# First attention of a decoder block: where the check of a top-32 selection is counted, and when sums are copied out

## The reference, cut to what matters

```python
Q = (x_text @ Wq).reshape(Bb, Tt, H, DH)          # 16 x 256 queries, 4 heads
K = (x_vision @ Wk).reshape(Bb, Gg, H, DH)        # 1601 keys
scores = jnp.einsum('bthd,bghd->bhtg', Q, K) / np.sqrt(DH).astype(np.float32)
topv, topi = jax.lax.top_k(scores, K_TOP)         # K_TOP = 32
probs = jax.nn.softmax(topv, axis=-1)
attn = jnp.zeros_like(scores).at[bi, hi, ti, topi].set(probs)
attn_mean = attn.mean(axis=1)                     # mean over the heads
V = x_vision @ Wv
c_t = jnp.einsum('btg,bgd->btd', attn_mean, V)    # then two FiLM products
```

## Time and profile before

| | us |
|---|---|
| median of 3 runs (lowest, highest) | 2802.61 (2799.21, 2804.65) |
| the profiled execution | 2799.72 |
| its span from first to last instruction | 2798.0 |
| PE, DVE, ACT, POOL busy over the span | 2382.1, 2183.1, 2102.0, 1531.4 |
| mean granted TensorE clock | 0.917 |

### The profile page before, as it was taken

One profiled execution on the slowest core, in us unless ns is written; L12 is line 12 of the kernel. 1 busy time (PEld: TensorE's weight loads), 2 busy tenths in 40 slices (PEclk: granted clock), 3 DMA queues, 4 the chain that ended last, 5 costly groups with the idle time before them and its releaser, 6 DMA issues. The chain is left out here.

```text
span 2798.0 us, 61626 instructions
## 1 busy us (share of the span) xinstructions
PE 2382.1 (85%) x19766; PEld 1236.7 (44%) x19766; DVE 2183.1 (78%) x7984; ACT 2102.0 (75%) x3544; POOL 1531.4 (55%) x2172
## 2 busy tenths in 40 slices
PE   7967888888888888865878849999999999999968
PEld 5634555555555555543542213333333333333348
DVE  8818888887888887834654579999999999999644
ACT  5739988988898998851522219999999989999935
POOL 1417778777787777752310043556556665543444
PEclk9968999988999999878978859999999999999989
DMA  8830000000000000018143023444443444433211
GB/s 246 266 102 1 14 14 16 23 14 16 14 14 14 14 14 14 14 50 290 31 63 85 20 73 96 95 108 107 107 104 98 102 99 98 104 88 55 74 46 45
DMA packets 163716, 199.26 MB, mean 71 GB/s; under 512 B 78966, under 2 KB 131740, under 8 KB 163376
## 3 DMA queue, kind: packets, MB, share of 16 engines
q1 hardware_dynamic: 153376, 157.34, 22.8%
q0 software_dynamic: 10000, 37.83, 3.9%
HBM read 133.22 MB, written 62.08 MB: 70 GB/s over the span
## 5 line engine op out<-in xcount | busy, mean ns | idle before, releaser
L2282 ACT ACTIVATE pb<-sps 128x512 f32<-128x512 f32 (+1 forms) x1664 | 897.9, 597 | 137.1 <-PE sps L2212 120.3
L2307 DVE TENSOR_REDUCE mx<-wps 128x2 f32<-128x1024 f32 x768 | 884.5, 1217 | 34.4 <-PE wps L2182 27.7
L1078 DVE MAX8 cand<-sc 128x8 f32<-128x46 f32 (+1 forms) x4480 | 603.0, 199 | 145.1 <-issue 82.1
L2227 PE MATMUL ops<-pb,va 128*9 128x256 f32 x6656 | 515.9, 382 | 9.5 <-issue 2.6
L854 PE MATMUL scores<-ctxT,qT 97*128 97x512 f32 (+1 forms) x1024 | 445.2, 584 | 81.5 <-ACT sc L966 69.5
L854 PEld LDWEIGHTS scores<-ctxT,qT 97*128 97x128 f32 x1024 | 208.6, 214 | 324.6 <-issue 224.7
L737 POOL TENSOR_TENSOR prf<-sc,prf 128x1601 f32<-128x1601 f32 x64 | 229.7, 3589 | 120.0 <-ACT prf L973 120.0
L737 POOL TENSOR_TENSOR prs<-sc,prs 128x1601 f32<-128x1601 f32 x64 | 230.7, 3604 | 18.6 <-ACT prs L973 15.7
L829 PE MATMUL misc<-diag,prs 128*128 128x128 f32 (+1 forms) x1664 | 227.8, 291 | 8.1 <-issue 6.9
L829 PEld LDWEIGHTS misc<-diag,prs 128*128 128x128 f32 (+1 forms) x1664 | 207.6, 199 | 18.5 <-issue 15.0
L2227 PEld LDWEIGHTS ops<-pb,va 128*9 128x9 f32 x6656 | 99.2, 88 | 253.6 <-ACT pb L2282 180.8
(11 more groups left out here) (476 smaller groups left out, 4233.6 us busy)
## 6 DMA issues: line engine op xcount, KB each, us to landing
FO<-keys SPq DMA_DIRECT2D x392, 50.0 KB
XX<-keys SPq DMA_DIRECT2D x392, 50.0 KB
ctxn<-in_ctx_dram SPq DMA_DIRECT2D x32, 576.0 KB
keys<-kpb POOLq DMA_DIRECT2D x42, 400.2 KB, 3.6
toep<-kernpad SPq DMA_DIRECT2D x8, 2048.0 KB, 15.0
values<-s_vs SPq DMA_DIRECT2D x16, 832.0 KB, 6.0
XX<-values SPq DMA_DIRECT2D x16, 832.0 KB, 4.7
keysf<-s_kf SPq DMA_DIRECT2D x16, 800.5 KB, 3.7
```

Source lines behind the costliest of these rows:

```text
L1078: st.add(v.max(cand[s % 2][:, 8 + n:8 + n + 7 * NP + 1:NP], sc[s % 4][:, c:c + w]))
L2227: ins = t.matmul(ops[VW * i:VW * i + DH1 + 1, 0:S], va[par][0:kn(kt), kt, 4 * g + i, :], pb[(UNITS * g + 2 * kt + i % 2) % 8][0:kn(kt), i ...
L2282: nc.scalar.activation(pb[(UNITS * g + u) % 8][0:rows_, :, :], sps[(UNITS * g + u) % SB][0:rows_, :, :], ACT.Exp).then_inc(p_ready, 1)
L2307: v.tensor_reduce(mx4[:, m // 2, :, 2 * g + m % 2, c], both, AX.X, ALU.max).then_inc(work_read, 1)
```

## The change

The sign pass on ACT is gone, and its buffers. DVE keeps three candidate buffers in place of two. After it has the threshold of slot j, it counts for slot j-1: how many of the 280 candidates (8 of each piece) reach the bound, and how many of the 35 pieces' eighth candidates do. PE adds both sums and takes 32 away for each row. So a row with 32 candidates at the bound and no piece whose eighth candidate reaches it gives zero. The bound has its sign turned on POOL.

ACT's copies of the weighted sums (t0 to t3) move from the step in which PE makes them to the next step, behind its clamp (`held_of`). The "!" moves to the front in the steps with such sums.

```diff
-        STEADY = (("!", "w"), ("q0", "!", "q1"), ("t0'", "!", "t1'"), ("f0'", "t2'", "!", "t3'"), ("!", "u1'"),
-                  ("f1'", "!", "c0", "c1", "c2", "c3"), ("t0", "!", "t1"), ("t2", "!", "t3"))
+        STEADY = (("!", "w"), ("q0", "!", "q1"), ("!", "t0'", "t1'"), ("!", "f0'", "t2'", "t3'"), ("!", "u1'"),
+                  ("f1'", "!", "c0", "c1", "c2", "c3"), ("!", "t0", "t1"), ("!", "t2", "t3"))
+        HELD = ("t0'", "t1'", "t2'", "t3'", "t0", "t1", "t2", "t3")
...
-            st.link(g.memset(plain[:, :], float(NK - 2 * TOPK)))
+            st.link(g.memset(plain[:, :], -float(TOPK)))
...
-                t.matmul(dps[0:1, 0:1], sides[:, s % 2:s % 2 + 1], onecol[:, :], start=True, stop=False)
+                for n in range(2):
+                    t.matmul(dps[0:1, 0:1], sides[:, s % 2, n:n + 1], onecol[:, :], start=(n == 0), stop=False)
...
-            def side_of(s, j):
-
-                act.wait_ge(below32_ready, j + 1)
-                if not isinstance(j, int) or j >= 2:
-                    act.wait_ge(doubts_ready, j - 1)
-                s_.activation(side[s % 2][:, :], sc[s % 4][:, :], ACT.Sign, bias=below32[:, s % 2:s % 2 + 1],
-                              accum_out=sides[:, s % 2:s % 2 + 1]).then_inc(sides_ready, 1)
...
+            def held_of(b, s):
+
+                for name in steps_of(b)[s]:
+                    if name in HELD:
+                        sums_out(bank(b, name), int(name[1]), number(b, name))
...
                         below_of(b if s else b - 1, (s - 1) % NS, j - 1)
-                        side_of((s - 1) % NS, j - 1)
+                        held_of(b if s else b - 1, (s - 1) % NS)
...
+            def counts_of(s, j, link):
+
+                dve.wait_ge(below32_ready, j + 1)
+                dve.sem_inc(slot_begun, 1)
+                low = below32[:, s % 2:s % 2 + 1]
+                for n, c in enumerate((cand[j % 3][:, 8:8 + 8 * NP], cand[j % 3][:, 8 + 7 * NP:8 + 8 * NP])):
+                    o = over_t[:, 8 * NP * n:8 * NP * n + (8 - 7 * n) * NP]
+                    (link if n else st.add)(v.tensor_scalar(o, c, low, 0.0, ALU.is_ge, ALU.add,
+                                                            accum_out=sides[:, s % 2, n:n + 1]))
+                dve.sem_inc(sides_ready, 1)
...
                     dve.sem_inc(thr_ready, 1)
+                    if not (first and s == 0):
+                        counts_of((s - 1) % NS, j - 1, link)
                     if s % 2 and not (first and s == 1):
                         add_pair((s - 2) % NS, j - 2, link, ahead)
```

More of the change, by code:

```diff
@@ L585, in attention0_phase @@
         FEW = 8 + RANKS * NP
-        cand = [sb(f"cand{i}", [P, 8 + 8 * NP]) for i in range(2)]
+        cand = [sb(f"cand{i}", [P, 8 + 8 * NP]) for i in range(3)]
         cleft = sb("cleft", [P, FEW])
-        side = [sb(f"side{i}", [P, NK], BF16) for i in range(2)]
-        sides = sb("sides", [P, 2])
+        over_t = sb("over_t", [P, 9 * NP], BF16)
+        sides = sb("sides", [P, 2, 2])
         onecol, plain = sb("onecol", [P, 1]), sb("plain", [P, 1])
@@ L730, in below32_of @@
                 st.link(g.tensor_scalar(e, t32, -1.0, t32, ALU.mult, ALU.max))
-                g.tensor_scalar(below32[:, s % 2:s % 2 + 1], e, 2.0 ** -22, t32, ALU.mult, ALU.subtract
+                g.tensor_scalar(below32[:, s % 2:s % 2 + 1], e, -(2.0 ** -22), t32, ALU.mult, ALU.add
                                 ).then_inc(below32_ready, 1)
@@ L1017, in step @@
                                 doubts_of((s - 1) % NS, j - 1)
+                            continue
+                        if name in HELD:
                             continue
@@ L1035, in _ @@
             below_of(B - 1, NS - 1, NS * B - 1)
-            side_of(NS - 1, NS * B - 1)
+            held_of(B - 1, NS - 1)
             doubts_of(NS - 1, NS * B - 1)
@@ L1073, in settle, with pieces_of @@
                 dve.sem_inc(settled, 1)
-            def pieces_of(s):
+            def pieces_of(s, j):
                 for n, (c, w) in enumerate(PIECES):
-                    st.add(v.max(cand[s % 2][:, 8 + n:8 + n + 7 * NP + 1:NP], sc[s % 4][:, c:c + w]))
+                    st.add(v.max(cand[j % 3][:, 8 + n:8 + n + 7 * NP + 1:NP], sc[s % 4][:, c:c + w]))
                     yield
+            def counts_of(s, j, link):
[7 more added lines that the diff above has]
+                dve.sem_inc(sides_ready, 1)
             def step(b, par, visit, first, last):
@@ L1083, in step @@
                     dve.wait_ge(scores_out, 1)
-                    for _ in pieces_of(0):
+                    for _ in pieces_of(0, 0):
                         pass
@@ L1093, in step @@
                         dve.sem_inc(slot_begun, 1)
-                        ahead = pieces_of((s + 1) % NS)
+                        ahead = pieces_of((s + 1) % NS, j + 1)
                     def link(ins):
@@ L1104, in step @@
                     tp = top[:, s % 4, :]
-                    x, y = cand[s % 2][:, 0:FEW], cleft[:, :]
+                    x, y = cand[j % 3][:, 0:FEW], cleft[:, :]
                     done = st.n
@@ L1110, in step @@
                         dve.wait_ge(dve_step, done)
-                    link(v.max(cand[s % 2][:, 0:8], cand[s % 2][:, FEW:8 + 8 * NP]))
+                    link(v.max(cand[j % 3][:, 0:8], cand[j % 3][:, FEW:8 + 8 * NP]))
                     for r in range(TOPK // 8):
@@ L1141, in _ @@
             walk(dve, step)
+            counts_of(NS - 1, NS * B - 1, st.link)
             settle(NS - 1, NS * B - 1)
```

## The result

The changed kernel takes 2865.34 us (median; 2861.77 to 2873.03), the kernel before 2800.91 beside it: a ratio of 1.0244, 95% interval 1.0224 to 1.0263. It is slower by some 64 us, where 27 were forecast. The profiled execution has a span of 2860.0 us.

What follows compares the result with a forecast made beforehand. ACT looked like the bound before, a loop through the engines after: 60.2 us a batch plus 4.2 low clock, 64.4 against 63.74. 2802.6 + 11 + 18.6 for the doubt = 2832, given as 2830 us; range 2782 to 2873.

Steps and rivals of the forecast that it cites:

- step 7 to 1: Pair sum to pair sum through DVE, PE, ACT and POOL: 15.77 us, plus 1.75 for slow context products.
- step 1 to 3: Pair sum to pair sum, set by DVE alone: 14.12 us, plus about 2.0 for slow sums of step 2.
- step 3 to 5: Like the first stretch with "u1'" in place of "w": 15.13 us, plus 0.5 for "u1'" at times slow.
- step 5 to 7: Pair sum to pair sum, set by POOL alone, its cut held 1.87 us by the pair sum: 15.20 us.
- Count latency: DVE's two added counting instructions in each slot: 0.6 us, between 0.4 and 0.8.
- Low clock: PE at 1.2 GHz after waits: "w" 1.75, sums of step 2 about 2.0, "u1'" 0.5; 4.2 us a batch.
- Low clock of the kernel before: The 61.80 us batch holds one slow run of scores, 4.71 for 2.9 us; without it 60.0.
- Pair sum held: Steps 1, 5, 7: DVE's pair sum starts when POOL's subtraction ends, and POOL's cut waits its 1.87 us.
- The new doubt: One row (batch 5, head 1, query 184) sends one slot through the general selection: 18.6 us on DVE, 15 to 21.
- Held copies: ACT's copies of weighted sums behind the next clamp hide most of 3.3 us a batch of waiting for PE.
- chain: Loop through the engines from pair sum to pair sum: 60.2 us a batch at 2.4 GHz, against 60.0 before.
- The rival of a worse clock: Most PE products after an idle are slow: 67 us a batch, 52 more, 2873 with the doubt; chance 0.11.

Runs made afterwards that it cites:

- idle products: Changed kernel with 4, 8, 3 and 4 unread 256-column products ahead of PE's wait for the count in steps 0, 2, 4, 6: 2783.60 us.
- the run without counts: Changed kernel without DVE's two counting instructions, doubts always zero, signal to PE still behind the last maximum: 2786.86 us.

## Why the prediction was wrong in size, and what of it held

Slower was right, and so was the mechanism: PE's queue stands behind a count that DVE makes late, and then runs at the low clock. The step that failed is the price of that clock. The forecast had 4.2 us a batch of it in the changed kernel against 3.7 in the kernel before, 0.5 more; the runs show 5.8 against 2.3, 3.5 more. That is some 50 us where 8 were forecast, and the batch takes 67.2 us in place of 64.4.

Stretches from pair sum to pair sum, read from DVE's timeline in 14 batches (of a held pair sum, its end less 1.87):

| us | forecast at 2.4 GHz + clock | changed kernel, mean | with idle products |
|---|---|---|---|
| step 7 to 1 | 15.77 + 1.75 | 17.51 (17.99 ten times, 16.32 four times) | 16.33 |
| step 1 to 3 | 14.12 + 2.0 | 16.70 | 14.65 to 15.0 |
| step 3 to 5 | 15.13 + 0.5 | 16.69 (17.16 ten times, 15.50 four times) | 15.50 |
| step 5 to 7 | 15.20 | 16.27 | 14.9 |
| batch | 64.4 | 67.2 | 61.4 |

- **Bound: right.** ACT no longer sets the time; the loop through DVE, POOL, ACT and PE does. At 2.4 GHz that loop is 61.4 us, 60.2 forecast, and no shorter than before, as forecast. In part that is luck: the kernel before was put at 60.0 and is at 61.4, so two errors of like size cancel, and the loop had no term for the 2.0 us a batch that the held copies alone bring.
- **Count latency: 0.6 forecast, 1.07 measured** from the end of the last maximum, 748.45, to PE's product at 749.52. The two instructions take 0.60 together (748.73 to 749.33), as forecast; 0.28 ahead of them (two pieces) and 0.19 from the start of the last reading to PE were not in the sum. The last column exceeds the forecast by 0.4 to 0.9 in the first three stretches, each of which has such a count in it; that this is the reason is argued, not tested.
- **Low clock: the mis-sized term.** The waits were seen well: 2.9 and 4.5 us estimated in steps 0 and 2, 2.82 and 4.69 in the rows above. What they cost, stretch by stretch (the third column less the fourth): "w" 1.2 a batch, 1.75 forecast, while the rest of its stretch was 0.56 too short, so that two errors cancel; the sums of step 2 about 2, as forecast; "u1'" 1.2, put at 0.5 from its wait of 1.3 (it waits 1.61 at 783.84 and ran slow ten times of 14); the sums of step 6 1.4, put at nothing, because that stretch was taken for POOL's alone. It is PE's and ACT's. After a wait of 2.24 us the sums are slow, ACT's copy, its exp and the pair sum follow them, and POOL's subtraction (ended at 809.17) is not what the pair sum waits for:

```profile
801.01 0.24 PE L864 MATMUL dps<-onecol,sides 128*1 128x1 f32 x4 [2.24 <-DVEq L1092]
...
801.23 5.47 PE L830 MATMUL misc<-diag,prs 128*128 128x128 f32 x32
...
806.73 0.59 ACT L949 COPY prT<-misc 128x512 f32<-128x512 f32 x1 [1.76 <-PE misc L830]
807.22 1.63 ACT L981 ACTIVATE prs<-prs,negm 128x1601 f32<-128x1601 f32 x1
...
810.40 1.87 DVE L1153 SCALAR_TENSOR_TENSOR prs<-prf,ratio,prs 128x1601 f32<-128x1601 f32 x1
```

- **Low clock of the kernel before: 2.3, not 3.7.** The forecast took one group of scores at the low clock off the 61.80 us batch and had 60.0. That batch has two groups at the low clock (484.20 and 497.49), and with idle products, where one is left, a batch still takes 61.4: most of that time was not on the path.
- **Pair sum held: right in steps 1 and 5, wrong in step 7.** 2.28 us beside the subtraction and then 1.75 for the cut, as forecast. In step 7 it came at 1870 ns, behind the subtraction, because of the slow sums of step 6: with the idle products, where these are fast, eleven of 14 pair sums of step 7 take 2.0 to 2.16 us. The Trainium skill, "SBUF — State Buffer", section "Who interferes with whom", has a DVE instruction with two SBUF inputs and a GpSimd instruction that reads SBUF shut each other out; the rows above agree for both orders. The run that put a wait in its place was 23 us slower.
- **The new doubt: right.** Once, in the batch named; 19.0 us on DVE (18.6 forecast), 15 to 16.6 in the time, near the lower end given.
- **Held copies:** 3.2 us a batch came without the late count (51 us in 16 batches, the moved "!" included), near the 3.3 that they were to hide; 31 us with the clock kept up (2763.50 to 2732.68). Beside the late count nothing of it was left.
- **Sum:** chain 3, clock 8, selection 19 were forecast; about 50 came from the clock, 15 to 20 from the selection, and what is left for the chain, 0 to 5, lies within the scatter of the runs. Without the selection the forecast was 11 us slower, so most of the forecast slowdown was the new doubt; without it the change is still slower by some 50 us, and that is the clock. The rival of a worse clock (67 us a batch, 2873), given 0.11, is the one that came.

## What to carry to other kernels

A signal that moves to a later engine costs most in what is queued behind it on the waiting engine: put independent work ahead of the wait, or make the signal earlier in the order of its own engine, before counting what the signal's work costs. When two kernels differ in how long PE stands, compare them once with PE kept busy on both sides; what remains is the chain, the rest is clock. A wait also has to be priced at each place where it stands, by what PE does behind it. And run the halves of a change apart: here one half was worth 51 us and the other hid it.

## What the runs showed of the hardware

- Products that nobody reads shortened the time: 2865 to 2784, 2796 to 2763, 2746 to 2733 us, with the granted clock of a whole batch at 0.97 to 1.00 in place of 0.87 to 0.95.
- The length of the last idle doesn't decide the clock by itself: in the run without counts the sums behind 1.70 us of standing took 5.47 us, and "w" behind 2.27 us took its 3.00 two steps later.
- A count over 280 elements with its sum takes 0.50 us on DVE against 0.26 for a maximum over 113, and reading the sum out is an instruction of its own (0.08 us).
